# Weight folding with four rows of PSUM, and the value weight folded between the first key tiles

## The reference

```
x = x + tanh(g_xattn[0]) * attention0(layernorm(x), ctx, ctx)    # 16 heads, 4 superposed parts, "interference"
x = x + tanh(g_ffn[0])   * (dense + low-rank update)(layernorm(x))
x = x + tanh(g_xattn[1]) * windowed_attention(layernorm(x), ctx)  # window of 16
x = x + tanh(g_ffn[1])   * clustered_dense(layernorm(x))
```

```
y = (x @ W.T + bias).reshape(b, s, H, dk, M)           # W is 1024 x 1024, for q, k and v
y = y + 0.1 * amp * einsum('bhsdi,hij->bhsdj', y, interference)
```

## Time and profile before

| | |
|---|---|
| three runs without profile | 2180.28, 2182.61, 2183.51 us (median 2182.61) |
| the profiled execution | 2183.45 us, of which the span of the trace is 2181.7 |
| PE, PEld, DVE, ACT, POOL busy | 91%, 73%, 49%, 30%, 17% of the span |
| mean granted TensorE clock | 0.954 of full speed |
| project_q, folding to the first product | from 20 to 44 us |
| project_kv, barrier to the first key tile | from 251 to 302 us |

### The profile page before, as it was taken

How to read it: one execution, slowest core, us unless ns; L and a number is a source line. 1 busy time by engine, 2 the same in 40 slices (tenths; PEclk the granted TensorE clock), 3 DMA queues, 4 the chain that set the end, 5 groups by cost and what they waited for, 6 DMA issues and landing times. The chain is left out here.

```text
span 2181.7 us, 50890 instructions
## 1 busy us (share of the span) xinstructions
PE 1979.2 (91%) x20126; PEld 1596.3 (73%) x20126; DVE 1069.1 (49%) x1866; ACT 660.6 (30%) x1114; POOL 370.4 (17%) x341
## 2 busy tenths in 40 slices
PE   6999689999995999999996799998698989986998
PEld 6999689999994777777774477776366666664887
DVE  5444231121113555555553555553678777854443
ACT  2222131111101443444432111121366656652000
POOL 0000000000005310111110000000465555640000
PEclk9999899999996999999998899999699999996999
DMA  4332434443347454445532345544755344423442
GB/s 149 117 115 97 174 116 167 148 143 114 113 162 303 181 202 185 174 184 213 212 126 88 112 169 183 185 175 164 185 145 146 117 140 124 124 80 110 145 147 90
DMA packets 149429, 328.60 MB, mean 151 GB/s; under 512 B 56432, under 2 KB 82672, under 8 KB 141104
## 3 DMA queue, kind: packets, MB, share of 16 engines
q1 hardware_dynamic: 147344, 326.04, 42.4%
q10 hardware_dynamic: 1952, 0.60, 0.1%
HBM read 200.25 MB, written 125.83 MB: 149 GB/s over the span
## 5 line engine op out<-in xcount | busy, mean ns | idle before, releaser
L1499 ACT ACTIVATE a_pt<-a_st_bank 128x1024 f32<-128x1024 f32 x128 | 131.1, 1024 | 267.9 <-PE a_st_bank L1545 267.9
L1051 POOL TENSOR_TENSOR a_sm<-a_sm,a_nmax 113x1024 f32<-113x1024 f32 x84 | 159.1, 1901 | 113.8 <-DVE a_nmax L1101 113.8
L1451 DVE TENSOR_REDUCE a_nmax<-a_s_bank 128x8 f32<-128x1024 f32 x128 | 156.5, 1223 | 27.6 <-PE a_s_bank L1533 21.2
L268 PE MATMUL q_qb<-q_xt_hi,wq_hi 128*128 128x256 f32 x512 | 146.2, 286 | 3.0 <-DVE wq_lo L179 3.0
L268 PE MATMUL kv_kb<-kv_ct_hi,wk_hi 128*128 128x256 f32 x512 | 144.9, 283 | 3.0 <-DVE wv_lo L179 3.0
L268 PE MATMUL q_qb<-q_xt_lo,wq_hi 128*128 128x256 f32 x512 | 145.6, 284 | 0.0
L268 PE MATMUL q_qb<-q_xt_hi,wq_lo 128*128 128x256 f32 x512 | 145.6, 284 | 0.0
L268 PE MATMUL kv_kb<-kv_ct_hi,wk_lo 128*128 128x256 f32 x512 | 144.9, 283 | 0.0
L268 PE MATMUL kv_kb<-kv_ct_lo,wk_hi 128*128 128x256 f32 x512 | 144.9, 283 | 0.0
L1228 PE MATMUL a_s_bank<-a_ks,a_qs 64*49 64x256 f32 x1344 | 98.2, 408 | 32.3 <-DMA a_ks<-k 20.2
L1095 DVE TENSOR_TENSOR a_sm<-a_s_bank,a_band 113x1024 f32<-113x1024 f32 x84 | 102.8, 1224 | 42.8 <-PE a_s_bank L1228 41.8
(11 more groups left out here) (203 smaller groups left out, 4517.1 us busy)
## 6 DMA issues: line engine op xcount, KB each, us to landing
a_qs<-q SPq DMA_DIRECT2D x32, 1024.0 KB, 5.4
a_ks<-k SPq DMA_DIRECT2D x32, 1024.0 KB, 7.2
k<-kv_raw SPq DMA_DIRECT2D x32, 512.0 KB, 4.5
f_xin<-x SPq DMA_DIRECT2D x32, 512.0 KB, 4.7
a_vraw<-v SPq DMA_DIRECT2D x32, 304.0 KB
q_xin<-in_x SPq DMA_DIRECT2D x16, 512.0 KB, 5.8
q<-q_out_lo SPq DMA_DIRECT2D x16, 512.0 KB, 3.6
q<-q_out_hi SPq DMA_DIRECT2D x16, 512.0 KB, 4.3
```

Source lines behind the costliest of these rows:

```text
L268: m = pe.matmul(out, a(x, c), b(y, c), start=(i + j == 0), stop=(len(terms) * j + i == n - 1))
L1051: pool.tensor_tensor(sm[live, k], sm[live, k], nmax[live, k, :].unsqueeze(2).to_broadcast([LIVE, 16, KEYS]), ALU.add).then_inc(shifted, 1)
L1451: dve.tensor_reduce(to, s_bank[:].rearrange("p b (h x) -> p b h x", h=4), X, ALU.max, negate=True).then_inc(maxed, 1)
L1499: act.activation(pt[:, s % 2], st_bank[:].rearrange("p b (h x) -> p (b h) x", h=4), ACT.Exp).then_inc(expd, 1)
```

## The change

Two things are changed, both in the folding.

First, `FoldedWeight` has no loops and no START any more. Its methods do one row `r` each, `banks` is a list of pairs of banks, and the numbers that are waited for are constants. The first rows wait for nothing but their own data: a load waits for `folded` only once the slots are used up, a fold waits for `lo_done` only once the banks are. Wq and Wk get four pairs of banks, so that four rows are in flight: Wq the banks `q_qb` and `q_tb` (from row 2 on PE waits until unit 0 has been copied out of `q_tb`), Wk all 8 banks. In `project_kv` the first four rows of Wk are loaded ahead of `kv_cin`, and ACT and DVE split them ahead of `inputs(0, 0)`.

Second, Wv is not folded ahead of the first key tile but in 8 pieces behind the 8 key tiles of unit 0, one row behind each tile, with two slots and two pairs of banks of its own (those of the value tiles). `kv_cin` of unit 1 is still loaded behind the last row of Wv. Unit 0 and unit 7 are now written out ahead of and behind the loop.

```diff
-    def load(self, sp):
-        w = self.src.rearrange("(o p) c -> o p c", p=P)
-        with sp.Fori(0, NC // RAW) as i:
-            for k in range(RAW):
-                sp.wait_ge(self.folded, free(self.base + RAW * i + k, RAW))
-                sp.dma_start(self.raw[:, k, :], w[RAW * i + k]).then_inc(self.loaded[k], 16)
-
-    def fold(self, pe, banks):
-        if not self.base:
-            begin(pe, self.folded)
-        with pe.Fori(0, NC // RAW) as i:
-            for k in range(RAW):
-                pe.wait_ge(self.loaded[k], 16 * (self.base // RAW + i + 1))
-                pe.wait_ge(self.lo_done, free(self.base + RAW * i + k))
...
+    def load(self, sp, r):
+        slots = self.raw.shape[1]
+        if r >= slots:
+            sp.wait_ge(self.folded, r - slots + 1)
+        sp.dma_start(self.raw[:, r % slots, :], self.rows[r]).then_inc(self.loaded[r % slots], 16)
+
+    def fold(self, pe, r):
+        slots, depth = self.raw.shape[1], len(self.banks)
+        pe.wait_ge(self.loaded[r % slots], 16 * (r // slots + 1))
+        if r >= depth:
+            pe.wait_ge(self.lo_done, r - depth + 1)
+        for c in range(NC):
+            m = pe.matmul(self.banks[r % depth][:, c // 4, c % 4 * P:(c % 4 + 1) * P],
+                          self.raw[:, r % slots, c * P:(c + 1) * P], self.e.fold[:, r, :], start=True, stop=True,
+                          skip_group_check=True)
+        m.then_inc(self.folded, 1)
...
@@ project_q
+        w = FoldedWeight(nc, ctx, e, "wq", e.i["Wq0"], sb("wq_raw", [P, RAW, D]),
+                         [qb[:, 0:2, :], qb[:, 2:4, :], tb[:, 0:2, :], tb[:, 2:4, :]], QS)
...
             def weights():
                 pe.wait_ge(biased, 1)
-                w.fold(pe, qb)
+                for r in range(NC):
+                    if r == 2:
+                        pe.wait_ge(xlo, done(1))
+                    w.fold(pe, r)
                 w.ready(pe)
...
@@ project_kv
+        banks = ps("kv_banks", [P, 8, 512])
+        kb, vb = banks[:, 0:4, :], banks[:, 4:8, :]
+        wk = FoldedWeight(nc, ctx, e, "wk", e.i["Wk0"], raw, [banks[:, 2 * k:2 * k + 2, :] for k in range(4)])
+        wv = FoldedWeight(nc, ctx, e, "wv", e.i["Wv0"], raw[:, 0:2, :], [vb[:, 0:2, :], vb[:, 2:4, :]])
...
+            for r in range(RAW):
+                wk.load(sp, r)
             load(0, 0, 0)
-            wk.load(sp)
-            wv.load(sp)
+            for r in range(RAW, NC):
+                wk.load(sp, r)
+            sp.wait_ge(wk.folded, NC)
+            for r in range(NC):
+                wv.load(sp, r)
             load(1, 1, 0)
...
@@ project_kv, DVE (ACT in the same way)
+            for r in range(RAW):
+                wk.split_lo(dve, r)
             inputs(0, 0)
-            wk.split_lo(dve, kb)
-            wv.split_lo(dve, kb)
-            one_ahead(dve, G, inputs, outputs, started=True)
+            for r in range(RAW, NC):
+                wk.split_lo(dve, r)
+            for o in range(NC):
+                keys_out(0, 0, o)
+                wv.split_lo(dve, o)
+            inputs(1, 1)
+            values_out(0, 0)
+            others(dve, inputs, outputs)
...
@@ project_kv, PE
-            wk.fold(pe, kb)
-            wv.fold(pe, kb)
-            wv.ready(pe)
...
+            for r in range(NC):
+                wk.fold(pe, r)
+            wk.ready(pe)
...
+            pe.wait_ge(clo, done(0))
+            for o in range(NC):
+                keys(0, 0, o)
+                wv.fold(pe, o)
+            wv.ready(pe)
+            values(0, 0)
```

More of the change, by code:

```diff
@@ L97, in begin, with __init__ @@
         eng.sem_inc(s, START)
[L100 to L111, removed]
 class FoldedWeight:
-    def __init__(self, nc, ctx, e, name, src, scale=1.0, share=None, raw=None):
+    def __init__(self, nc, ctx, e, name, src, raw, banks, scale=1.0):
         sb, ps, sem = scope(nc, ctx)
-        self.e, self.src, self.scale = e, src, scale
+        self.e, self.rows, self.scale = e, src.rearrange("(o p) c -> o p c", p=P), scale
         self.hi = sb(f"{name}_hi", [P, NC, D], F32R)
         self.lo = sb(f"{name}_lo", [P, NC, D], F32R)
[L124 to L130, removed]
+        self.raw, self.banks = raw, banks
+        self.loaded = [sem(f"{name}_loaded{k}") for k in range(raw.shape[1])]
         self.folded = sem(f"{name}_folded")
@@ new lines, in _views, with split_hi, split_lo @@
+    def _views(self, r, h):
+        v = self.banks[r % len(self.banks)][:, h, :].rearrange("p (c o) -> p c o", c=4)
+        at = (slice(None), slice(4 * h, 4 * h + 4), slice(r * P, r * P + P))
+        return v, self.hi[at], self.lo[at]
+    def split_hi(self, act, r):
+        act.wait_ge(self.folded, r + 1)
+        for h in range(2):
+            v, hi, _ = self._views(r, h)
+            a = act.activation(hi, v, ACT.Copy, scale=self.scale)
+        a.then_inc(self.hi_done, 1)
+    def split_lo(self, dve, r):
+        dve.wait_ge(self.hi_done, r + 1)
+        for h in range(2):
+            v, hi, lo = self._views(r, h)
+            a = dve.scalar_tensor_tensor(lo, v, self.scale, hi.bitcast(F32), ALU.mult, ALU.subtract)
+        a.then_inc(self.lo_done, 1)
@@ L528, in project_kv, with others @@
         ctx_t = e.i["ctxT"].rearrange("(c p) t -> p c t", p=P)
+        def others(eng, inputs, outputs):
+            with eng.Fori(0, (G - 2) // 2) as i:
+                for g in (1, 2):
+                    inputs(2 * i + g + 1, 1 - g % 2)
+                    outputs(2 * i + g, g % 2)
+            outputs(G - 1, 1)
         by_batch = lambda a: a.rearrange("p (b t) -> p b t", b=2)
@@ L595, in outputs @@
                 for o in range(NC):
-                    act.wait_ge(mm, done(NC * g + o))
-                    act.activation(k_hi[:, :, o, :], by_batch(kb[:, o % 4, 0:2 * P]), ACT.Identity,
-                                   bias=e.bkf[:, o:o + 1]).then_inc(khi, 1)
+                    keys_out(g, s, o)
+            for r in range(RAW):
+                wk.split_hi(act, r)
             inputs(0, 0)
-            wk.split_hi(act, kb)
-            wv.split_hi(act, kb)
-            one_ahead(act, G, inputs, outputs, started=True)
+            for r in range(RAW, NC):
+                wk.split_hi(act, r)
+            for o in range(NC):
+                keys_out(0, 0, o)
+                wv.split_hi(act, o)
+            inputs(1, 1)
+            others(act, inputs, outputs)
         @block.tensor
@@ L625, in product @@
                                      range(NC)).then_inc(vmm, 1)
-            with pe.Fori(0, G // 2) as i:
-                for s in range(2):
-                    product(2 * i + s, s)
+            def product(g, s):
+                pe.wait_ge(clo, done(g))
+                for o in range(NC):
+                    keys(g, s, o)
+                values(g, s)
+            pe.wait_ge(clo, done(0))
+            for o in range(NC):
+                keys(0, 0, o)
+                wv.fold(pe, o)
+            wv.ready(pe)
+            values(0, 0)
+            with pe.Fori(0, (G - 2) // 2) as i:
+                product(2 * i + 1, 1)
+                product(2 * i + 2, 0)
+            product(G - 1, 1)
 def staggered(eng, units, per_loop, stages, between=None, at=0, started=(), opening=None):
```

76 lines of the change are left out of this document (27 added, 49 removed).

## The result

The changed kernel took 2166.52 us (median of 4 runs, 2165.14 to 2170.08), the kernel before 2181.86 beside it: ratio 0.9932, 95% interval 0.9918 to 0.9945. So the change takes 14 to 15 us. The forecast was 2171.

The account below looks back on a forecast made before the run. PE, busy 91% of the span, bounds the kernel. 4.6 + 7.0 = 11.6 us off the profiled 2183.45 gives 2171.9, stated as a median of 2171; range 2165 to 2177, the forecast's own 2168 to 2174 (65%).

Parts of the forecast that it names:

- Project_q: Early Wq loads and four rows in flight: first product at 39.2 against 43.83, 4.6 us less, bounds 3.5 and 5.7.
- Both unknowns: In project_q: seams between rows, 0.6 us taken of 1.2; row 0 at half clock, 0.5 taken of 1.0.
- Project_kv, up to the first key tile: PE starts 3.5 us behind SP's first issue; DVE is late next; first key tile at 275.9, 25.9 us earlier.
- rival D: In project_kv DVE's queue of input and four rows holds the first key tile: gain 7 to 8, 2175; chance 5%.
- Tiles and rows: Wv's rows among unit 0's key tiles: 4.74 us for a tile and a row, seams 0.7 in all, loads in time.
- rival C: Slower: PE at half clock among the tiles, deciding against the change from 8 falls of 1.6 us on; chance 4%.
- The stall at the end: Behind Wv's last row PE waits again for ACT and DVE: a new stall of 3.2 us ahead of the values.
- The clock: Falls behind three stalls, before two: from -1.6 to +3.2 us; one fall, as before, held likeliest, so nothing taken.
- rival A: All three stalls followed by clock falls, seams at 0.17, Wq's row 0 at half rate: gain 6.6, 2176; chance 12%.
- From unit 1 on: In project_kv nothing differs but one loop round less; no gain taken.
- The sum 4.6 + 7.0: 4.6 us from project_q plus 7.0 from project_kv up to the start of values, 11.6 in all.
- rival E: More gain: no seams, no falls, full clock at once: 15.8 us, 2167; chance 9%.

Follow-up runs that it names:

- kv_only: Only project_kv changed, project_q that of the kernel before: 2177.56 us, ratio 0.9987 to the kernel before.
- whole: The changed kernel again, nothing altered, measured and profiled a second time: 2166.10 us against 2180.53 for the kernel before, ratio 0.9940.
- q_only: Only project_q changed, project_kv that of the kernel before: 2181.54 us, ratio 1.0007 to the kernel before.
- the directive: One more line ahead of PE's loop in the second attention, with offset 0 or 128, no work changed; on the kernel before: 2183.22 us, ratio 1.0012.
- fill: The changed kernel with Wv's first two rows folded behind Wk and none behind the last two key tiles: 2159.19 us, ratio 0.9898 to the kernel before.
- before_pin: The kernel before with the directive at offset 0: 2183.22 us, ratio 1.0012 to the kernel before.
- depth2_pin: The changed kernel with the directive, Wq and Wk with two pairs of banks in place of four: 2176.34 us, ratio 0.9981 to the kernel before.
- q_only_pin: Only project_q changed against the kernel before, with the directive at offset 0: 2182.36 us, ratio 1.0003 to the kernel before.
- the one with 128: The changed kernel with the directive at offset 128 instead of 0: 2165.64 us, ratio 0.9927 to the kernel before.

## Why the prediction was right, and where it was off

**Project_q: right in kind, 1.7 us too small.** Start of the fold 20.06 for 20.0 forecast; the banks of the transposes cost nothing, as forecast. Both unknowns came out at nothing: no seam between rows (0.6 reckoned) and row 0 at full rate (0.5). A row is 1.79 us from start to start, not its own 1.86 (8 rows 14.4 for 14.9). The end is 3.0 for 3.2. 6.3 gained where 5.7 was my upper bound; that bound had used a row's duration where the distance between starts is what adds up (0.5), and 3.2 for the end (0.2). That row 0 ran at full rate, and no load was late, holds for this profile; above are others with neither.

**Project_kv, up to the first key tile: right by two errors.** PE started 4.45 us behind SP's first issue, not 3.5. That is not mainly the four rows in flight: `kv_only` issues the same four and starts after 3.67. The other 0.8 go with the new project_q, as said above, and could not be seen in the rows of before. The input landed 11.2 behind that issue (9.7 reckoned), at 256.5; ACT came to it only at 260.98, so it cost nothing, and rival D has no place. DVE was late next, as forecast, and ended the input 19.9 behind the issue, where 18.7 was reckoned; but it did the four rows behind it in 4.87, not 5.6. First key tile 24.8 behind the issue (24.6): that the two agree so well is luck.

**Tiles and rows: right.** 4.67 us for a tile and a row, where 4.74 was forecast, no seam, no wait for a load, clock 1.00 over 28 us: rival C is refuted. The stall at the end is 2.5 for 3.2.

**The clock: wrong in the profiled execution.** I forecast one fall, as before, and there were three. That is what rival A named, but with seams at 0.17 and row 0 at half rate, which did not come. Values started 5.9 earlier by the stage's own time instead of 7.0: the first key tiles at half rate cost 2.8, without which it would be 8.7. In `whole` the clock did not fall at project_q's first product, the first key tiles were at half rate in part only, and the values not at all. So this term has no fixed value, it is a spread. Windows of `whole` at the two places in project_kv:

```profile
268.80:275.00 6.20, 6.18 (x42) 6.18 (x43) 0.48 (x1) 0.48 (x1) 0.00 (x0) 0.77 0.19 77
310.10:320.00 9.90, 9.86 (x43) 8.18 (x44) 2.98 (x2) 0.46 (x1) 0.00 (x0) 1.00 0.60 201
```

**From unit 1 on: nothing, as reckoned.** From the first value product to the end of project_kv it is 340.6 us before (from 324.9 on) and 342.4 after, 340.7 without its fall of the clock. Stages behind project_kv differ by 0.0, 1.9 and 1.2 us, and by 1.0, 4.8 and 0.1 between the two profiles of the changed kernel.

The sum 4.6 + 7.0 stands against 6.2 + 9.4 clock-free. The mechanisms were right; both sums were low. In project_q it is the two unknowns (1.1) and the row's distance (0.5). In project_kv, up to the values, it is seams that don't exist (0.7), the stall at the end (0.7) and the row's distance (0.5), less 0.2 at the first key tile; that is 1.7 of the 2.4, and the rest is within what the clock-free values are good for. The medians, 2166.1 and 2166.5, lie in the range of 2165 to 2177 but below the forecast's own 2168 to 2174; only the profiled run's 2170 is inside that. They are at rival E's 2167, whose "no seams" came true, and "no falls" in part. The forecast's 11.6 was 3 to 4 us short, and the wide range, not the sum, made it hold.

What I did not foresee is that the parts don't add. The gain of 15.6 can be followed in the stages of both profiles of the changed kernel, but `q_only` shows none of its 6 in the medians. For that I have the slower first load (1.3), the second attention (6 clock-free, in code that the part does not change), and the clock; with the directive the loss there is gone from the profile, but not from the median, and that is open.

## What to carry to other kernels

Look at what PE does between two dense stretches: a fold, a cast or a split that goes through two other engines wants enough pairs of banks to cover its chain (four did here, two did not), loads that are issued ahead of every counter, and the last pieces spread among work that doesn't need them. A stall of 3 us can cost nearly twice its length, since the clock may fall behind it (3.1 and then 2.8 us in one profile here, less in another); closing both stalls (`fill`) gave 7 to 8 us where they were 5.6. An experiment that undoes one part keeps the layout of the others, so its loss need not be that part's gain. And compare two kernels by medians over many runs, or stage by stage with the half-rate time taken out: two profiles of one kernel were 8 us apart.

## What the runs showed of the hardware

- One kernel, two executions: 101.8 and 82.9 us of PE work at half rate, spans 2168.3 and 2160.3. Behind the same stall of 3 us the granted clock was 0.50 in one, 0.77 in the other.
- Idle pieces of 0.96 to 1.24 us behind each pair of rows (project_q of before, `before_pin` and `depth2_pin`) were never seen to lower it: 1.00 from 26.96 to 40.60 us in before, from 28.6 to 42.0 in `before_pin`, from 24.4 to 37.4 in `depth2_pin`. Two rows behind them took 3.65 to 3.68 where they ran without a seam. Behind a stall of 2.5 us it fell in one profile (0.52) and not in another (1.00).
- 16 weight loads and matmuls of 128 columns take 1.79 us from start to start, and waits for constants add nothing: in the changed kernel pairs of rows start at 23.69, 27.27 and 30.84. With loops and registers a pair of rows at the same depth took 4.89 in before and 4.88 in `before_pin`, against 4.61; in before a seam of 0.17 stands between the rows, in `before_pin` none, and the wait behind the pair is longer instead (1.24).
- A load of 1 MB as the first transfer behind the barrier took 5.3 us in before and `before_pin`, and 6.5 and 6.6 in `q_only` and `q_only_pin` (not explained). Behind four loads of 512 KB it took 9.4 in the changed kernel; these took 5.6 (median), where the first row of Wq in before took 3.3.
- PE stops of 0.5 to 4.6 us with no semaphore inside the long loop of the second attention, 10 to 15 us a pass. The two longest stand at the same instruction in all 14 profiles. The two next stand at PE's matmuls 498 and 623 of the stage in all seven kernels with offset 0, and at 311 and 436 in the one with 128.
